# Pseudo-inverse of 128 landmark matrices on one core: one 64x64 tensor tile per head in place of block diagonals of two heads

## The chip, the cores and the metric

The kernel runs on one core of one Trainium2 chip. The metric is the time of one execution on the device in microseconds (us). The core's engines are TensorE (PE, its weight loads are listed apart as PEld), VectorE (DVE), ScalarE (ACT), GpSimd (POOL) and SyncE (SP, which here only starts transfers).

## The reference

The whole program is a two-dimensional LSTM over 16 images of 64x64 positions with 128 channels, then an attention layer with 64 landmarks and 8 heads of 16 channels, then a recurrent layer. The part that matters here is the pseudo-inverse of the landmark attention, one 64x64 matrix for each of 16 x 8 = 128 heads:

```python
def moore_penrose_pinv(x, iters=6):
    abs_x = jnp.abs(x)
    col = abs_x.sum(axis=-1).max()
    row = abs_x.sum(axis=-2).max()
    z = jnp.swapaxes(x, -1, -2) / (col * row)
    I = jnp.eye(x.shape[-1], dtype=x.dtype)
    for _ in range(iters):
        xz = x @ z
        z = 0.25 * z @ (13.0 * I - xz @ (15.0 * I - xz @ (7.0 * I - xz)))
    return z
attn2_inv = moore_penrose_pinv(attn2)
out = attn1 @ attn2_inv @ (attn3 @ v)
```

All of it is fp32. The maxima behind col and row go over all 128 heads.

## The kernel before

The program is a chain of phases, each an own block in which every engine has its own instruction queue: group norm, LSTM, landmark phase, pseudo-inverse (`pinv_phase`, L1080), output phase, recurrence. Engines wait for each other by semaphores alone, and the order on each engine is written out by hand.

`pinv_phase` holds the 128 matrices as NP = 64 pairs: partitions 0 to 63 carry the first head of a pair, 64 to 127 the second. They are worked on in NCH = 8 chunks of PCH = 8 pairs, so that a chunk of 64 columns per pair fills one bank of the matmul memory (PSUM). `bank` has four such banks, `wide` two times two for products of 128 columns per pair.

A matmul takes its weights over all 128 partitions. To multiply two heads in one 128x128 product, their matrices must stand on the diagonal of a 128x128 matrix that is otherwise zero. `diag_p` and `diag_t` are those matrices; `blocks(diag, c, h)` (L1136) is the part of a chunk that belongs to one head. Both are cleared at the start (L1153 on POOL, L1260 on DVE) and filled by copies, head by head.

Ahead of the rounds, in order: POOL makes `zeros` and `halves` (L1154 to L1158), and SP stores the zeros and eight diagonals for the next phase; TensorE sums the columns (L1169), DVE takes row sums and maxima (L1272 to L1276); ACT copies x into diag_p (L1235), TensorE turns it (L1179), ACT stores xT (L1239), DVE copies it into diag_t (L1280); POOL reduces the maxima over the partitions (L1160), DVE forms `inv` (L1286); TensorE multiplies xT by itself (L1188), ACT scales the product into `pz[..., 0, :]` (L1243) and x into `pz[..., 1, :]` (L1244), DVE copies the first into diag_p (L1291).

`pz` holds two matrices per head, P (which is x z) and a form of z, side by side in 128 columns. Each of the six rounds (PINV_ITERS, a loop on every engine) has three stages of eight chunks:

- stage 1: DVE forms 7 I - P in `tm` (L1300), TensorE multiplies by diag_p into `bank` (L1204);
- stage 2: DVE forms 15 I minus the bank in `tm` (L1303), TensorE multiplies by diag_p again (L1204);
- stage 3: DVE forms 3.25 I minus a quarter of the bank, in two instructions, straight into diag_t (L1307); TensorE multiplies both halves of pz by it into `wide` (L1215); ACT copies the result back to pz in two instructions per chunk (L1251) and its first half into diag_p in two more (L1255).

A stage's chunk c waits for the bank's reader four chunks earlier, and in stage 3 for ACT's copy of chunk c - 2. The copy into diag_p releases the next round's stage 1 by the semaphore s_pd. Behind the rounds TensorE multiplies each head's z by its context, with 64x64 weights and 16 columns, head by head (L1226), and DVE copies the result (L1312). Then the next phase's block begins.

Of the kernel before, what the change touches and what calls it, by code (L numbers as in the profile page):

```python
# [11 lines left out]
P = 128  # L12
# [1058 lines left out]
PCH = 8  # L1071
# [8 lines left out]
def pinv_phase(nc, sems, R, band, taps):  # L1080
# [7 lines left out]
    with ExitStack() as ctx:  # L1088
# [4 lines left out]
        diag_p = m.sb("i_diag_p", [P, NP, 2 * LM])  # L1093
        diag_t = m.sb("i_diag_t", [P, NP, 2 * LM])
# [16 lines left out]
        s_zero = sems.sem("i_zero")  # L1111
        s_zeros = sems.sem("i_zeros")
        s_band = sems.sem("i_band")
        s_xd = sems.sem("i_xd")
        s_xtd = sems.sem("i_xtd")
        s_pd = sems.sem("i_pd")
# [6 lines left out]
        s_pass = sems.sem("i_pass")  # L1123
# [11 lines left out]

        def blocks(diag, c, h):  # L1136
            return diag[HEAD[h], chunk[c], LM * h:LM * h + LM]
# [14 lines left out]
        def _(pool):  # L1152
            pool.memset(diag_p[:, :, :], 0.0).then_inc(s_zero, 1)  # L1153
# [9 lines left out]
        def _(pe):  # L1163
# [8 lines left out]
            for c in range(NCH):  # L1172
# [4 lines left out]
                pe.wait_ge(s_xd, c + 1)  # L1177
                for j in range(PCH):
                    mt = nc.tensor.matmul(bank[c % 4][:, j, :], diag_p[:, PCH * c + j, :], eye[1.0][:, :], start=True, stop=True)  # L1179
                mt.then_inc(s_x, 1)  # L1180

            for c in range(NCH):

                pe.wait_ge(s_xc, NCH + c - 3)
                pe.wait_ge(s_xtd, c + 1)
                for j in range(PCH):
                    n = PCH * c + j
                    mt = nc.tensor.matmul(bank[c % 4][:, j, :], diag_t[:, n, :], xT[:, n, :], start=True, stop=True)  # L1188
                mt.then_inc(s_x, 1)

            def iteration(k):
                for stage in range(2):
                    for c in range(NCH):


                        at = 3 * NCH * k + NCH * stage
                        pe.wait_ge(s_t, at + NCH + c - 3 if c >= 4 else at + c + 1 + 4 * stage)
                        pe.sem_inc(s_pass, 1)
                        if stage == 0:
                            pe.wait_ge(s_pd, NCH * k + c + 1)  # L1200
                            pe.sem_inc(s_pass, 1)
                        for j in range(PCH):
                            n = PCH * c + j
                            mt = nc.tensor.matmul(bank[c % 4][:, j, :], diag_p[:, n, :], tm[:, n, :], start=True, stop=True)  # L1204
                        mt.then_inc(s_q, 1)
                for c in range(NCH):
                    pe.wait_ge(s_t, 3 * NCH * k + 2 * NCH + c + 1)
                    pe.sem_inc(s_pass, 1)

                    pe.wait_ge(s_new, NCH * (k + 1) + c + 1)  # L1210
                    pe.sem_inc(s_pass, 1)
                    for j in range(PCH):
                        n = PCH * c + j
                        out = wide[c % 2][j // 4][:, j % 4, :, :].rearrange("p a l -> p (a l)")
                        mt = nc.tensor.matmul(out, diag_t[:, n, :], pz[:, n, :, :].rearrange("p a l -> p (a l)"),  # L1215
                                              start=True, stop=True)
                    mt.then_inc(s_pz, 1)
            pe.wait_ge(s_xc, 2 * NCH)
            with pe.Fori(0, PINV_ITERS) as k:
                iteration(k)  # L1220
# [976 lines left out]
```

## Time and profile before

| | us |
|---|---|
| median of 3 runs | 6811.03 |
| lowest and highest | 6809.58, 6813.49 |
| the profiled execution | 6810.61 |
| its span | 6808.7 |

The span goes from the first instruction to the last. Busy shares of the span are TensorE 91%, its weight loads 55%, VectorE 45%, ScalarE 47% and GpSimd 27%. The profile puts the pseudo-inverse at about 2674 to 3042 us of the span. Times in rows are us, or ns where a row says mean ns. "Idle before" is the time in which an engine stood still just ahead of the instructions of a group, with what ended it. PEclk is the clock that TensorE was granted as a share of 2.4 GHz. A matmul of fp32 appears as two weight loads and two matmul instructions, so that the 64 pairs of a stage are 128 of each. Rows name tiles without their numbers, and the form 64*64 is the rows and columns of the array that an instruction uses.

### The profile page before, as it was taken

Reading aid. Unit: us, or ns where it says so; the run is one execution under the profiler, and the core shown is the slowest. Engines: PE = TensorE matmul, PEld = TensorE weight load, DVE = VectorE, ACT = ScalarE, POOL = GpSimd, SP = SyncE. Lnnn points to the kernel's source line nnn. Section 1 sums busy time; section 2 is a strip of 40 time slices with the busy share of each in tenths; the row PEclk is TensorE's granted clock in tenths of the full one; section 3 lists DMA queues with packets and bytes.
Section 4 is the critical chain, followed back from the end, with each engine's and each line's share of the span. In section 5 each row is a group of like instructions: output and inputs, shape, how many; then the busy total and the mean of one; then the engine's idle time right before and its main releaser. Section 6 shows DMA issues by size and latency. Waiting matters only on the chain. (4 is left out here: it accounts for less than half of the span.)

```text
span 6808.7 us, 240684 instructions
## 1 busy us (share of the span) xinstructions
PE 6191.8 (91%) x100325; PEld 3736.2 (55%) x100560; DVE 3093.8 (45%) x8331; ACT 3215.1 (47%) x9215; POOL 1857.0 (27%) x2255
## 2 busy tenths in 40 slices
PE   4499999997888887989999999979999999999999
PEld 3499888995666665983444444433333333333333
DVE  7677777775777765434666666610000000000000
ACT  4366555564666664334555555523333333333333
POOL 1000000004767762005777777710000000000000
PEclk6699999998999999898999999989999999999999
DMA  6631112125766661014555555411111211211111
GB/s 265 257 115 67 69 50 75 58 102 178 218 216 205 206 201 38 0 33 127 154 155 154 155 157 154 127 54 44 55 44 43 56 43 43 56 43 47 52 44 42
DMA packets 785139, 715.35 MB, mean 105 GB/s; under 512 B 68336, under 2 KB 662256, under 8 KB 781040
## 3 DMA queue, kind: packets, MB, share of 16 engines
q1 hardware_dynamic: 769712, 599.13, 28.7%
q0 software_dynamic: 14400, 101.45, 3.7%
q8 instruction: 776, 12.71, 0.8%
q14 instruction: 251, 2.06, 0.1%
HBM read 390.60 MB, written 307.89 MB: 103 GB/s over the span
## 5 line engine op out<-in xcount | busy, mean ns | idle before, releaser
L2096 PE MATMUL f_junk<-f_idle 128*32 128x384 bf16 x24736 | 1566.7, 323 | 2.4 <-issue 2.4
L2139 ACT ACTIVATE f_y<-f_acc 128x16 f32<-128x16 f32 x4096 | 753.7, 184 | 1553.8 <-PE f_acc L2107 1553.8
L2107 PEld LDWEIGHTS f_acc<-f_y,f_vT 128*32 128x32 f32 x32768 | 649.2, 108 | 1412.1 <-ACT f_y L2139 1401.1
L2107 PE MATMUL f_acc<-f_y,f_vT 128*32 128x16 f32 x32768 | 1049.7, 193 | 58.0 <-issue 9.5
L2054 DVE TENSOR_TENSOR f_sum<-f_turned,f_t 128x512 f32<-128x512 f32 x128 | 88.5, 691 | 1762.9 <-PE f_turned L2089 1762.9
L1826 DVE TENSOR_REDUCE o_m<-o_bank_l 128x8 f32<-128x512 f32 x512 | 325.6, 678 | 382.0 <-remote 372.8
L2096 PEld LDWEIGHTS f_junk<-f_idle 128*32 128x32 bf16 x24736 | 447.0, 96 | 4.5 <-issue 4.2
L399 ACT ACTIVATE l_gate<-l_pf,l_bf 128x256 f32<-128x256 f32 (+12 forms) x768 | 273.4, 407 | 229.0 <-PE l_pf L374 228.4
L336 POOL DMA_DIRECT2D hidden<-l_h x48 | 36.2, 754 | 1256.9 <-DVE l_hsum L453 1191.9
L916 ACT ACTIVATE a_p<-a_s 128x512 f32<-128x512 f32 x512 | 264.3, 602 | 194.0 <-PE a_s L807 194.0
L365 PE MATMUL l_pf<-l_x,l_wf 128*128 128x256 f32 (+12 forms) x1536 | 317.9, 330 | 36.7 <-DMA l_x<-skew 36.7
L1792 ACT ACTIVATE o_p<-o_bank_s 128x512 f32<-128x512 f32 x512 | 264.4, 602 | 88.2 <-PE o_bank_s L1647 88.2
L365 PEld LDWEIGHTS l_pf<-l_x,l_wf 128*128 128x128 f32 x1536 | 253.0, 191 | 52.4 <-issue 36.8
L402 ACT ACTIVATE l_tanhc<-l_cell 128x256 f32<-128x256 f32 (+12 forms) x384 | 137.3, 358 | 277.3 <-DVE l_cell L429 277.3
L976 DVE TENSOR_REDUCE a_m3p<-a_s 128x1 f32<-128x512 f32 x384 | 238.2, 682 | 53.4 <-remote 51.8
L2044 DVE TENSOR_SCALAR f_wxn<-f_wx,f_scale,f_shift 128x2048 f32<-128x2048 f32 x32 | 84.9, 2652 | 384.3 <-DMA f_wx<-wx 344.2
L2089 PE MATMUL f_turned<-f_ident,f_y 128*32 128x128 f32 x4096 | 224.3, 292 | 1.7 <-issue 1.5
L2078 PE MATMUL f_acc<-f_wxn,f_ident 128*32 128x128 f32 x4096 | 211.1, 278 | 15.2 <-DVE f_wxn L2044 13.3
L701 POOL TENSOR_TENSOR a_r<-a_vare,a_half 128x8 f32<-128x8 f32 x128 | 209.6, 1638 | 10.0
L434 DVE TENSOR_TENSOR l_h<-l_gate,l_tanhc 128x256 f32<-128x256 f32 (+12 forms) x384 | 134.3, 350 | 163.0 <-ACT l_tanhc L402 163.0
L1204 PE MATMUL i_bank<-i_tm,i_diag_p 128*128 128x64 f32 x1536 | 198.3, 299 | 2.7 <-DVE i_tm L1300 2.7
L1204 PEld LDWEIGHTS i_bank<-i_tm,i_diag_p 128*128 128x128 f32 x1536 | 198.0, 215 | 2.8 <-issue 2.8
(253 smaller groups left out, 12939.2 us busy)
## 6 DMA issues: line engine op xcount, KB each, us to landing
a_hid<-hidden SPq DMA_DIRECT2D x112, 520.0 KB, 4.6
hidden<-l_h POOLq DMA_DIRECT2D x48, 1040.0 KB, 6.4
skew<-gn_skew POOLq DMA_DIRECT2D x8, 6144.0 KB, 23.8
l_x<-skew SPq DMA_DIRECT2D x48, 1024.0 KB, 5.2
vals<-a_v SPq DMA_DIRECT2D x128, 272.0 KB, 3.0
o_v<-vals SPq DMA_DIRECT2D x128, 272.0 KB, 3.5
gn_x<-in_x SPq DMA_DIRECT2D x16, 2048.0 KB, 12.4
a_xin<-in_x SPq DMA_DIRECT2D x128, 256.0 KB, 4.4
```

Of the source, the lines that this page charges most:

```text
L365: mm = nc.tensor.matmul(banks[c][g][:, :, rows], w[W[g]][:, :], xs, start=g in (0, 2, 3), stop=False, skip_group_check=True)
L399: nc.scalar.activation(gate[c][:, g, :, rows], banks[c][g][:, :, rows], ACT.Tanh if g == 2 else ACT.Sigmoid, bias=bias[BI[g]][:, 0:1]).the ...
L916: nc.scalar.activation(p3[c % 2][g][:, :], S[g][:, :], ACT.Exp).then_inc(s["exp"], 1)
L976: nc.vector.tensor_reduce(m3p[:, g, c:c + 1], bank[:, :], AX.X, ALU.max).then_inc(s["mx"], 1)
L1204: mt = nc.tensor.matmul(bank[c % 4][:, j, :], diag_p[:, n, :], tm[:, n, :], start=True, stop=True)
L1792: nc.scalar.activation(p1[g][:, :], bank_s[g][:, :], ACT.Exp).then_inc(s["exp"], 1)
L1826: nc.vector.tensor_reduce(m1[:, k, :].rearrange("p (g r) -> p g r", r=QUAD)[:, :, 0:2], bank_l[k % 2][:, :].rearrange("p (g a l) -> p g a ...
L2078: mm = nc.tensor.matmul(acc[k % 2][rows, PT * piece:PT * piece + PT, :], ident[:, rows], wxn[q][:, at, :], start=piece == 0, stop=False, s ...
L2089: mt = nc.tensor.matmul(turned[g % 2][rows, b % 4, :], y[q][:, rows, b], ident[:, :], start=True, stop=True)
L2096: nc.tensor.matmul(junk[rows, :], idle[:, 0:QUAD], idle[:, :], start=True, stop=True)
L2107: mm = nc.tensor.matmul(acc[k % 2][rows, t, :], vT[:, rows], before, start=False, stop=True, skip_group_check=True)
L2139: nc.scalar.activation(y[q][:, u, :], acc[u // RC % 2][:, u % RC, :], ACT.Sigmoid).then_inc(s_y, 1)
```

## The change

The diagonals go. Each product of a pair becomes two matmuls, one for each head, whose weights are 64x64: the first head uses rows 0 to 63 and columns 0 to 63 of the array, the second the other rows and columns. The weights are read directly from x, xT, pz and a new tile `tq`. All clearings and copies of the diagonals and their semaphores (s_zero, s_xd, s_xtd, s_pd, and s_pass) are removed; stage 1 waits for ACT's copy of pz (s_new) in place of s_pd. DVE's third instruction of a round becomes one over 128 partitions. The loops over rounds on the three engines are written out, and the last round forms only the second half of pz (`first`).

```diff
@@ -1090,8 +1090,7 @@
         xT = m.sb("i_xT", [P, NP, LM])
         pz = m.sb("i_pz", [P, NP, 2, LM])
         tm = m.sb("i_tm", [P, NP, LM])
-        diag_p = m.sb("i_diag_p", [P, NP, 2 * LM])
-        diag_t = m.sb("i_diag_t", [P, NP, 2 * LM])
+        tq = m.sb("i_tq", [P, NP, LM])
...
@@ -1150,7 +1141,6 @@
 
         @block.gpsimd
         def _(pool):
-            pool.memset(diag_p[:, :, :], 0.0).then_inc(s_zero, 1)
             pool.memset(zeros[:, :, :], 0.0).then_inc(s_zeros, 1)
             pool.memset(halves[:, :], 0.0).then_inc(s_const, 1)
             pool.wait_ge(s_const, 1)
@@ -1174,50 +1164,46 @@
                     pe.wait_ge(s_col, NCH + c - 3)
                 else:
                     pe.wait_ge(s_xc, c - 3)
-                pe.wait_ge(s_xd, c + 1)
                 for j in range(PCH):
-                    mt = nc.tensor.matmul(bank[c % 4][:, j, :], diag_p[:, PCH * c + j, :], eye[1.0][:, :], start=True, stop=True)
+                    for h in HEAD:
+                        mt = nc.tensor.matmul(bank[c % 4][h, j, :], x[h, PCH * c + j, :], eye[1.0][h, :], start=True, stop=True)
                 mt.then_inc(s_x, 1)
 
             for c in range(NCH):
 
                 pe.wait_ge(s_xc, NCH + c - 3)
-                pe.wait_ge(s_xtd, c + 1)
                 for j in range(PCH):
                     n = PCH * c + j
-                    mt = nc.tensor.matmul(bank[c % 4][:, j, :], diag_t[:, n, :], xT[:, n, :], start=True, stop=True)
+                    for h in HEAD:
+                        mt = nc.tensor.matmul(bank[c % 4][h, j, :], xT[h, n, :], xT[h, n, :], start=True, stop=True)
                 mt.then_inc(s_x, 1)
 
-            def iteration(k):
+            pe.wait_ge(s_xc, 2 * NCH)
+            for k in range(PINV_ITERS):
                 for stage in range(2):
                     for c in range(NCH):
 
-
                         at = 3 * NCH * k + NCH * stage
                         pe.wait_ge(s_t, at + NCH + c - 3 if c >= 4 else at + c + 1 + 4 * stage)
-                        pe.sem_inc(s_pass, 1)
                         if stage == 0:
-                            pe.wait_ge(s_pd, NCH * k + c + 1)
-                            pe.sem_inc(s_pass, 1)
+                            pe.wait_ge(s_new, 2 + NCH * k + c + 1)
                         for j in range(PCH):
                             n = PCH * c + j
-                            mt = nc.tensor.matmul(bank[c % 4][:, j, :], diag_p[:, n, :], tm[:, n, :], start=True, stop=True)
+                            for h in HEAD:
+                                mt = nc.tensor.matmul(bank[c % 4][h, j, :], pz[h, n, 0, :], tm[h, n, :], start=True, stop=True)
                         mt.then_inc(s_q, 1)
+                first = 1 if k == PINV_ITERS - 1 else 0
                 for c in range(NCH):
                     pe.wait_ge(s_t, 3 * NCH * k + 2 * NCH + c + 1)
-                    pe.sem_inc(s_pass, 1)
 
                     pe.wait_ge(s_new, NCH * (k + 1) + c + 1)
-                    pe.sem_inc(s_pass, 1)
                     for j in range(PCH):
                         n = PCH * c + j
-                        out = wide[c % 2][j // 4][:, j % 4, :, :].rearrange("p a l -> p (a l)")
-                        mt = nc.tensor.matmul(out, diag_t[:, n, :], pz[:, n, :, :].rearrange("p a l -> p (a l)"),
-                                              start=True, stop=True)
+                        for h in HEAD:
+                            mt = nc.tensor.matmul(wide[c % 2][j // 4][h, j % 4, first:2, :].rearrange("p a l -> p (a l)"),
+                                                  tq[h, n, :], pz[h, n, first:2, :].rearrange("p a l -> p (a l)"),
+                                                  start=True, stop=True)
                     mt.then_inc(s_pz, 1)
-            pe.wait_ge(s_xc, 2 * NCH)
-            with pe.Fori(0, PINV_ITERS) as k:
-                iteration(k)
 
             pe.wait_ge(s_new, 2 + NCH * (PINV_ITERS + 1))
             for n in range(NP):
@@ -1229,11 +1215,6 @@
         @block.scalar
         def _(act):
             act.sem_inc(s_new, 2)
-            act.wait_ge(s_zero, 2)
-            for c in range(NCH):
-                for h in range(2):
-                    mc = nc.scalar.activation(blocks(diag_p, c, h), x[HEAD[h], chunk[c], :], ACT.Identity)
-                mc.then_inc(s_xd, 1)
             for c in range(NCH):
                 act.wait_ge(s_x, NCH + c + 1)
                 nc.scalar.activation(xT[:, chunk[c], :], bank[c % 4][:, :, :], ACT.Identity).then_inc(s_xc, 1)
@@ -1243,21 +1224,17 @@
                 nc.scalar.activation(pz[:, chunk[c], 0, :], bank[c % 4][:, :, :], ACT.Identity, scale=inv[:, 0:1]).then_inc(s_xc, 1)
                 nc.scalar.activation(pz[:, chunk[c], 1, :], x[:, chunk[c], :], ACT.Identity, scale=inv[:, 0:1]).then_inc(s_new, 1)
 
-            with act.Fori(0, PINV_ITERS) as k:
+            for k in range(PINV_ITERS):
+                first = 1 if k == PINV_ITERS - 1 else 0
                 for c in range(NCH):
                     act.wait_ge(s_pz, NCH * k + c + 1)
                     for h in range(2):
                         lo = PCH * c + 4 * h
-                        mc = nc.scalar.activation(pz[:, lo:lo + 4, :, :], wide[c % 2][h][:, :, :, :], ACT.Identity)
+                        mc = nc.scalar.activation(pz[:, lo:lo + 4, first:2, :], wide[c % 2][h][:, :, first:2, :], ACT.Identity)
                     mc.then_inc(s_new, 1)
-                    act.wait_ge(s_new, 2 + NCH * (k + 1) + c + 1)
-                    for h in range(2):
-                        mc = nc.scalar.activation(blocks(diag_p, c, h), pz[HEAD[h], chunk[c], 0, :], ACT.Identity)
-                    mc.then_inc(s_pd, 1)
 
         @block.vector
         def _(dve):
-            nc.vector.memset(diag_t[:, :, :], 0.0).then_inc(s_zero, 1)
             steps = 0
 
             def step(ins):
@@ -1274,27 +1251,16 @@
             for c in range(NCH):
                 dve.wait_ge(s_x, c + 1)
                 nc.vector.tensor_reduce(cmax[:, c:c + 1], flat(bank[c % 4][:, :, :]), AX.X, ALU.max).then_inc(s_col, 1)
-            for c in range(NCH):
-                dve.wait_ge(s_xc, c + 1)
-                for h in range(2):
-                    mc = nc.vector.tensor_copy(blocks(diag_t, c, h), xT[HEAD[h], chunk[c], :])
-                mc.then_inc(s_xtd, 1)
             dve.wait_ge(s_col, NCH)
             step(nc.vector.tensor_reduce(top[:, 1:2], cmax[:, :], AX.X, ALU.max))
             dve.wait_ge(s_all, 1)
             step(nc.vector.tensor_tensor(prod[:, :], tops[:, 0:1], tops[:, 1:2], ALU.mult))
             step(nc.vector.reciprocal(inv[:, :], prod[:, :]))
 
-            for c in range(NCH):
-                dve.wait_ge(s_xc, NCH + c + 1)
-                for h in range(2):
-                    mc = nc.vector.tensor_copy(blocks(diag_p, c, h), pz[HEAD[h], chunk[c], 0, :])
-                mc.then_inc(s_pd, 1)
-
-            def both(k, rows=slice(0, P)):
-                return eye[k][rows, :].unsqueeze(1).broadcast_to([rows.stop - rows.start, PCH, LM])
-
-            with dve.Fori(0, PINV_ITERS) as k:
+            def both(k):
+                return eye[k][:, :].unsqueeze(1).broadcast_to([P, PCH, LM])
+
+            for k in range(PINV_ITERS):
                 for c in range(NCH):
                     dve.wait_ge(s_new, 2 + NCH * k + c + 1)
                     nc.vector.tensor_tensor(tm[:, chunk[c], :], both(7.0), pz[:, chunk[c], 0, :], ALU.subtract).then_inc(s_t, 1)
@@ -1303,10 +1269,8 @@
                     nc.vector.tensor_tensor(tm[:, chunk[c], :], both(15.0), bank[c % 4][:, :, :], ALU.subtract).then_inc(s_t, 1)
                 for c in range(NCH):
                     dve.wait_ge(s_q, 2 * NCH * k + NCH + c + 1)
-                    for h in range(2):
-                        mc = nc.vector.scalar_tensor_tensor(out=blocks(diag_t, c, h), in0=bank[c % 4][HEAD[h], :, :], scalar=-0.25,
-                                                            in1=both(3.25, HEAD[h]), op0=ALU.mult, op1=ALU.add)
-                    mc.then_inc(s_t, 1)
+                    nc.vector.scalar_tensor_tensor(out=tq[:, chunk[c], :], in0=bank[c % 4][:, :, :], scalar=-0.25,
+                                                   in1=both(3.25), op0=ALU.mult, op1=ALU.add).then_inc(s_t, 1)
             dve.wait_ge(s_z, 1)
             for q in range(2):
                 nc.vector.tensor_copy(c3[:, 32 * q:32 * q + 32, :].rearrange("p n d -> p (n d)"),
```

## Rows read from the trace of the kernel before

**Rows 1.** The page's first lines: span, and busy time with its share and instructions.

```profile
span 6808.7 us, 240684 instructions
PE 6191.8 (91%) x100325; PEld 3736.2 (55%) x100560; DVE 3093.8 (45%) x8331; ACT 3215.1 (47%) x9215; POOL 1857.0 (27%) x2255
```

**Rows 2.** Timeline at both ends of the phase: start, duration, engine, line, operation, count, idle before.

```profile
2673.93 6.93 POOL L1153 MEMSET i_diag_p<- 128x8192 f32 x1 [49.07 <-POOLq L502]
2675.72 6.88 DVE L1260 MEMSET i_diag_t<- 128x8192 f32 x1 [2.07 <-issue]
...
2682.78 10.10 PE L1169 MATMUL i_bank<-r_attn,i_halves 128*128 128x512 f32 x16 [9.60 <-POOL i_halves L1158]
...
2692.71 14.40 PE L1179 MATMUL i_bank<-i_eye,i_diag_p 128*128 128x64 f32 x128
...
2709.83 0.69 ACT L1243 ACTIVATE i_pz<-i_bank,i_inv 128x512 f32<-128x512 f32 x1 [2.09 <-DVE i_inv L1286]
...
2711.03 0.68 ACT L1243 ACTIVATE i_pz<-i_bank,i_inv 128x512 f32<-128x512 f32 x1
...
2724.13 2.16 PE L1204 MATMUL i_bank<-i_tm,i_diag_p 128*128 128x64 f32 x9 [2.73 <-DVE i_tm L1300]
...
3040.95 1.29 DVE L1312 COPY r_ctx<-i_bank 128x512 f32<-128x512 f32 x2 [30.98 <-PE i_bank L1226]
```

**Rows 3.** Groups by line and form, 2675.5 to 3042 us; the first line names the columns.

```profile
line engine op names shapes xcount | busy us, mean ns | idle before us <-releasers
L1204 PE MATMUL i_bank<-i_tm,i_diag_p 128*128 128x64 f32 x1536 | 198.3, 299 | 2.7 <-DVE i_tm L1300 2.7
...
L1215 PE MATMUL i_wide<-i_pz,i_diag_t 128*128 128x128 f32 x768 | 95.2, 280 | 9.9 <-ACT i_pz L1251 9.3
...
L1307 DVE SCALAR_TENSOR_TENSOR i_diag_t<-i_bank,i_eye 64x512 f32<-64x512 f32 x96 | 66.1, 689 | 36.9 <-PE i_bank L1204 36.2
L1255 ACT ACTIVATE i_diag_p<-i_pz 64x512 f32<-64x512 f32 x96 | 60.4, 629 | 2.1
L1251 ACT ACTIVATE i_pz<-i_wide 128x512 f32<-128x512 f32 x96 | 52.1, 594 | 192.4 <-PE i_wide L1215 191.4
L1300 DVE TENSOR_TENSOR i_tm<-i_eye,i_pz 128x512 f32<-128x512 f32 x48 | 32.6, 691 | 69.0 <-ACT i_pz L1251 69.0
...
L1226 PE MATMUL i_bank<-r_ctx,i_pz 64*64 64x16 f32 x256 | 12.5, 251 | 2.7 <-ACT i_pz L1251 2.7
```

**Rows 4.** Chosen stretches with busy time and granted clock; the first line names the columns.

```profile
core 0: us, PE busy (x) PEld busy (x) DVE busy (x) ACT busy (x) POOL busy (x), PEclk, DMA share, GB/s
...
2724.20:2778.60 54.40, 54.40 (x256) 54.40 (x256) 18.80 (x29) 0.00 (x0) 0.00 (x0) 0.50 0.00 1
2778.80:2785.20 6.40, 6.40 (x49) 6.39 (x48) 2.07 (x3) 3.29 (x6) 0.00 (x0) 0.83 0.01 3
2798.00:2823.00 25.00, 25.00 (x226) 25.00 (x225) 13.95 (x22) 3.03 (x6) 0.00 (x0) 1.00 0.00 0
...
3030.20:3040.80 10.60, 10.60 (x202) 10.60 (x200) 0.00 (x0) 0.00 (x0) 0.00 (x0) 0.50 0.01 2
3063.40:3090.80 27.40, 27.40 (x45) 4.98 (x46) 0.00 (x0) 4.18 (x7) 0.00 (x0) 0.50 0.36 97
```

**Rows 5.** Timeline of two chunks of stage 3, and of the final product.

```profile
2787.89 2.02 PE L1215 MATMUL i_wide<-i_pz,i_diag_t 128*128 128x128 f32 x16 [0.39 <-ACT i_pz L1251]
...
2790.30 2.02 PE L1215 MATMUL i_wide<-i_pz,i_diag_t 128*128 128x128 f32 x16 [0.39 <-ACT i_pz L1251]
...
3028.42 12.48 PE L1226 MATMUL i_bank<-r_ctx,i_pz 64*64 64x16 f32 x256 [2.71 <-ACT i_pz L1251]
```

**Rows 6.** Timeline of the landmark phase: four tiles side by side.

```profile
2657.63 1.06 PE L807 MATMUL a_s<-a_qbd,a_kT 32*128 32x128 f32 x32
2658.62 1.10 PE L821 MATMUL a_pv<-a_p,a_v 128*32 128x64 f32 x64
```

More of the change, by code:

```diff
@@ L1110, in pinv_phase @@
         zeros = m.sb("i_zeros", [P, HEADS, BAND])
-        s_zero = sems.sem("i_zero")
         s_zeros = sems.sem("i_zeros")
         s_band = sems.sem("i_band")
-        s_xd = sems.sem("i_xd")
-        s_xtd = sems.sem("i_xtd")
-        s_pd = sems.sem("i_pd")
         s_x = sems.sem("i_x")
@@ L1122, in pinv_phase @@
         s_new = sems.sem("i_new")
-        s_pass = sems.sem("i_pass")
         s_z = sems.sem("i_z")
@@ L1134, in pinv_phase @@
         HEAD = [slice(0, LM), slice(LM, 2 * LM)]
-        def blocks(diag, c, h):
-            return diag[HEAD[h], chunk[c], LM * h:LM * h + LM]
         @block.sync
```

## The prediction

> **What bounds the kernel now.** The span is 6808.7 us, TensorE is busy for 91% of it, and one core runs the phases one after another [rows 1]. The change touches the pseudo-inverse alone, which lies between DVE's clearing of a diagonal tile at 2675.72 and the two copies of the result at 3040.95 [rows 2], 365 us or 5.4% of the span. Whatever moves inside moves the end by as much, because the next phase starts behind it and does the same work. So the first view is the list of groups by line in this stretch [rows 3], then the stretches with the granted clock [rows 4], then the timeline [rows 2, 5, 6].
>
> The list says who works: L1204 (two of the three stages of a round) and L1215 (the third) keep TensorE busy for 198.3 and 95.2 us, with 2.7 and 9.9 us of idle time [rows 3]. From the first L1204 (2724.13) to L1226 (3028.42) it is 304.3 us [rows 2, 5]. In a stage of L1204, TensorE is the bound. A product of fp32 is two instructions, so a stage is 64 pairs x 2 = 128 of them, and they follow at 25.00 us / 224 = 0.112 us with a clock of 1.00 (226 less the two in progress at an edge), and at 54.40 / 256 = 0.213 us with 0.50 [rows 4]: 14.3 and 27.2 us a stage. In a stage of L1215 the matmuls would take 14.3 us too, but a chunk comes only every 2.41 us (2787.89 to 2790.30) [rows 5], because ACT makes two copies of 0.594 and then two into the diagonal of 0.629 us per chunk [rows 3]: ACT is the bound there, 8 x 2.41 = 19.3 us.
>
> The clock is the second thing to see. After TensorE's pause of 2.7 us [rows 3] ahead of the rounds it was granted 0.50, that is 1.2 of 2.4 GHz, and stayed there through the first two stages, 54.4 us without a gap; it rose as soon as L1215 ran (mean 0.83 in 2778.8 to 2785.2), and then stayed at 1.00 in L1204 as well [rows 4].
>
> **Stages 1 and 2 of a round.** Each pair's product of 128x128 by 64 becomes two of 64x64 by 64, in different rows and columns of the array: 256 instructions in place of 128. The nearest row is L1226, already in this form but with 16 columns. There 202 instructions stand in 10.60 us at clock 0.50 [rows 4]; less the four in progress that is 99 pairs, 0.107 us for the two heads together. At clock 1.00 the row is L821, four tiles with 64 columns side by side: 64 instructions in 1.10 us, of which 0.22 is the tail of the last, so 16 slots (15 gaps) of 0.058 us [rows 6]. A slot holds one pass of both heads, and a stage has 128: 128 x 0.058 = 7.4 us at the high clock, 128 x 0.107 = 13.7 us at the low. This halves the stage at either clock, since 64 columns of weights are loaded in place of 128.
>
> **Stage 3.** Here each head streams 128 columns, so the slot is bound by the stream. L807 has this width with four tiles: 32 instructions in 1.06 us, 0.27 of it tail, so seven gaps of 0.112 [rows 6]. The stage is 14.3 us at the high clock, and at the low 128 x 0.213 = 27.2 us. ACT's two diagonal copies are gone, which leaves two of 0.594 = 1.2 us per chunk under TensorE's 1.8: the ACT bound goes and TensorE is next. In the last round the left half is dropped: 64 columns, 7.4 or 13.7 us. DVE has 0.69 us per chunk and stage (the third now one instruction over 128 partitions in place of two over 64, same elements per partition, 0.689 each) [rows 3], under the 0.93 of a chunk of 16 slots; no new wait. At the turn of a round DVE's first stage waits for ACT's last copy, about 2.1 us behind the last L1215, and the fifth chunk, which needs DVE beyond that, starts only 3.7 us behind: hidden. If that cover went, it would cost about 1 us a round.
>
> **Rounds, summed.** High clock: 5 x (7.4 + 7.4 + 14.3) + 3 x 7.4 = 167.7 us; with some 5 us at the low clock first and small seams, 171.5. That is 132.8 less than 304.3. Low clock throughout: 5 x (13.7 + 13.7 + 27.2) + 3 x 13.7 = 314.1 us, 9.8 more than now.
>
> **Before the rounds.** TensorE's first product waits for POOL's small constants, queued behind the clearing of diag_p, and starts at 2682.78 [rows 2]. Without it they are ready some 6.8 us sooner: 2676.0 (bounds: nothing gained beyond DVE's own start at 2675.72, and 1.5 us lost if other work ends later). The products of L1169 take 9.9 us as now, to 2685.9. The transposes (L1179, 128 instructions in 14.40 us [rows 2]) take 128 x 0.058 = 7.5, to 2693.4. In the next step (L1188) ACT is late: its two scaled copies per chunk follow at 2711.03 - 2709.83 = 1.20 us [rows 2] against 0.93 on TensorE, so the last is done at 2694.5 + 7 x 1.20 + 0.69 = 2703.6. The 16+16+16 copies into diagonals and two clearings lie off this path. Rounds start at 2703.7, not 2724.13: 20.4 us gained (bounds 14 and 24). The price is a pause of about 4 us for TensorE ahead of the rounds, longer than the 2.7 us after which the clock was low; so I take it that the rounds start at the low clock again.
>
> **Behind the rounds.** The pause of 2.7 us before L1226 [rows 3], mostly ACT's queue, shrinks to 1.0: 1.7 gained. L1226 itself (12.48 us [rows 5]) is unchanged; with the clock high a little longer I take 11, between 7.5 and 13.7: 1.5 gained. The rounds written out take more code; TensorE ran L1179 and L1226 from straight code without a gap, so nothing for that (bounds 0 and 3 us). Fewer copies on ACT, DVE and POOL gain nothing else.
>
> **Forecast.** Profiled time 6810.6 - 20.4 - 132.8 - 1.7 - 1.5 = 6654.2; the median of the runs is 0.4 above the profiled one, so 6655 us. It stands on the clock rising early in the rounds.
>
> **Rival 1: the clock stays low.** Nothing here shows what two 64x64 tiles side by side do to the clock. For a rise: in the new stages both tiles stream nearly all the time (64 columns streamed while 64 weights load), where the old L1204 streamed half the time. Against: together they fill half the array, now in stage 3 too, and that was the stage that raised the clock. In 3063.4 to 3090.8 TensorE alternated full 128x512 matmuls with pairs of 32x32 tiles, was never idle, and kept 0.50 for 27.4 us [rows 4], so streaming alone does not do it; whether rows, columns or their product count, those rows leave open. If it stays low: 6810.6 - 20.4 + 9.8 - 1.7 + 1.2 (L1226 all low) = 6799.5, within 0.2% of now. The Trainium skill, TensorE: Matmul & The Clock Gate, Part 1, says that the clock goes by how busy TensorE has been of late, idle time lowering it and activity raising it. By that alone the forecast would be sure; the 54.4 us at 0.50 with no idle time [rows 4] speak against so simple a reading.
>
> **Rival 2: the heads go one after another, and it is slower.** L1226's tiles stream 16 columns, a small part of a slot, so its rows do not prove that two long streams into the same bank overlap. L807 writes four banks; L821 writes one bank from tiles in different columns with all rows. If the two heads' streams excluded each other, each slot would double: 1664 x 0.058 (13 stages of 128 slots) + 640 x 0.112 (5 stages) = 168 us in the rounds and 14 in the steps before. That gives 6655 + 182 = 6837 with the high clock, and more with the low. It decides for slower from 156/182 = 86% of the doubling on. The Trainium skill, TensorEngine Tiling (Array Packing), Gotcha 1: PSUM Pressure, has this rule: different row tiles cannot access the same PSUM bank at the same time. The two heads are different row tiles and share a bank, in different partitions; L1226 shows starts in pairs at one slot [rows 4], which speaks against it.
>
> **Rival 3: the clock wavers**, rising in some rounds only: about 6720 us.
>
> **How the numbers follow.** Forecast 0.50, rival 1 0.38, rival 2 0.05, rival 3 0.03; 0.04 for rival 1 with 2304 slots each over 0.011 us dearer, which alone would pass 6824. The forecast's own range is 6642 to 6672; rival 1's is 6793 to 6812. To hold eight in ten the range must take in both: 6642 to 6812. About 0.2%, 13.6 us, is what a measurement of this kernel can tell from no change. Faster by more: 0.50 + 0.03 and part of rival 1's lower end, 0.55. Within: 0.36. Slower: 0.09.
>
> **What would show it.** The first stages' slots in the new profile: 0.058 us (two instructions each) and a clock of 1.00 for the forecast, 0.107 and 0.50 for rival 1; starts of the two heads apart by a whole stream for rival 2. Stage 3: chunks 1.8 us apart, with ACT idle between. Rounds starting some 28 us behind the phase's start. A wait of TensorE for DVE within stages 1 and 2 would make the prediction wrong in a way that I have not priced.

## The result, and the profile after

The changed kernel takes 6652.85 us (median of four runs, 6649.13 to 6655.99) against 6810.31 for the kernel before in the same comparison: a ratio of 0.9771, with a 95% interval of 0.9757 to 0.9786. The forecast was 6655. The profiled execution took 6654.42 us, its span is 6652.8.

The first lines of the page, as [rows 1]:

```profile
span 6652.8 us, 245191 instructions
PE 6083.1 (91%) x103120; PEld 3601.9 (54%) x103120; DVE 3042.8 (46%) x8250; ACT 3140.9 (47%) x9103; POOL 1851.7 (28%) x2254
```

155.9 us of span are gone, and TensorE's share is the same 91%, which by itself says nothing. The groups by line of the pseudo-inverse are the answer to [rows 3]. L1193 is the old L1204, L1203 the old L1215, L1233 the old L1251, L1266 and L1272 the old L1300 and L1307, L1212 the old L1226.

```profile
line engine op names shapes xcount | busy us, mean ns | idle before us <-releasers
L1193 PE MATMUL i_bank<-i_tm,i_pz 64*64 64x64 f32 x3072 | 90.6, 218 | 2.6 <-ACT i_pz L1224 2.6
...
L1203 PE MATMUL i_wide<-i_pz,i_tq 64*64 64x128 f32 x1280 | 70.7, 269 | 0.0
L1233 ACT ACTIVATE i_pz<-i_wide 128x512 f32<-128x512 f32 x80 | 43.4, 594 | 101.9 <-PE i_wide L1203 101.9
L1266 DVE TENSOR_TENSOR i_tm<-i_eye,i_pz 128x512 f32<-128x512 f32 x48 | 33.3, 693 | 59.3 <-ACT i_pz L1233 47.8 <-ACT i_pz L1225 11.5
L1272 DVE SCALAR_TENSOR_TENSOR i_tq<-i_bank,i_eye 128x512 f32<-128x512 f32 x48 | 33.2, 692 | 11.6 <-PE i_bank L1193 11.6
...
L1212 PE MATMUL i_bank<-r_ctx,i_pz 64*64 64x16 f32 x256 | 10.4, 232 | 0.7 <-ACT i_pz L1233 0.7
...
L1203 PE MATMUL i_wide<-i_pz,i_tq 64*64 64x64 f32 x256 | 8.3, 219 | 0.0
```

Twice as many instructions of stages 1 and 2 (3072 for 1536) take 90.6 us in place of 198.3, of which 54.4 were at the low clock [rows 4]. No engine holds TensorE up inside the rounds: its only idle time is the 2.6 us ahead of them and the 0.7 behind. VectorE's third instruction over 128 partitions costs the same 0.69 us as each of the two over 64 partitions did, so a chunk of stage 3 saves one of the two.

The stretches with the granted clock, as [rows 4]:

```profile
core 0: us, PE busy (x) PEld busy (x) DVE busy (x) ACT busy (x) POOL busy (x), PEclk, DMA share, GB/s
2703.20:2717.80 14.60, 14.60 (x506) 14.60 (x504) 10.81 (x16) 0.36 (x1) 0.00 (x0) 1.00 0.02 4
2718.20:2732.00 13.80, 13.80 (x258) 13.80 (x256) 5.30 (x8) 7.59 (x14) 0.00 (x0) 1.00 0.01 2
...
2872.00:2875.50 3.50, 3.50 (x126) 3.50 (x125) 0.00 (x0) 0.00 (x0) 0.00 (x0) 1.00 0.00 0
2876.00:2881.80 5.80, 5.80 (x114) 5.80 (x112) 0.00 (x0) 0.00 (x0) 0.00 (x0) 0.50 0.00 0
```

A slot is, as in the prediction, the time for one instruction of each head. In stages 1 and 2, 506 instructions less some eight in progress are 249 pairs in 14.60 us: 0.0586 us a slot. In stage 3, 258 less four are 127 pairs in 13.80 us: 0.109. Read start by start, the second head's instruction of stages 1 and 2 begins 0.006 to 0.007 us behind the first head's, and the next pair 0.051 to 0.052 us later, so the two do run together. The clock is at 1.00 from the first instruction of the rounds to their end, where the kernel before had 54.4 us at 0.50 [rows 4]. It falls to 0.50 in the final product, whose pairs of 64x64 tiles stream 16 columns, without any idle time there.

The timeline, as [rows 2, 5], with two chunks of stage 3 on ScalarE:

```profile
2673.26 1.38 POOL L1144 MEMSET i_zeros<- 128x1536 f32 x1 [49.07 <-POOLq L502]
...
2675.24 10.05 PE L1159 MATMUL i_bank<-r_attn,i_halves 128*128 128x512 f32 x16 [2.75 <-POOL i_halves L1148]
...
2685.22 7.68 PE L1169 MATMUL i_bank<-i_eye,r_attn 64*64 64x64 f32 x256
...
2692.74 7.63 PE L1178 MATMUL i_bank<-i_xT 64*64 64x64 f32 x256
...
2703.00 15.15 PE L1193 MATMUL i_bank<-i_tm,i_pz 64*64 64x64 f32 x512 [2.63 <-ACT i_pz L1224]
...
2725.18 1.08 ACT L1233 ACTIVATE i_pz<-i_wide 128x512 f32<-128x512 f32 x2 [0.66 <-PE i_wide L1203]
2726.93 1.08 ACT L1233 ACTIVATE i_pz<-i_wide 128x512 f32<-128x512 f32 x2 [0.66 <-PE i_wide L1203]
...
2871.58 10.45 PE L1212 MATMUL i_bank<-r_ctx,i_pz 64*64 64x16 f32 x256 [0.75 <-ACT i_pz L1233]
2882.07 1.29 DVE L1276 COPY r_ctx<-i_bank 128x512 f32<-128x512 f32 x2 [18.64 <-PE i_bank L1212]
```

| part | before | after | difference | forecast |
|---|---|---|---|---|
| POOL's first instruction to the first round | 50.2 | 29.7 | -20.5 | -20.4 |
| rounds, with the wait behind them | 304.3 | 168.6 | -135.7 | -134.5 |
| the final product, to DVE's copy | 12.5 | 10.5 | -2.0 | -1.5 |
| all else | | | +2.3 | 0 |

The last line is the rest up to the 155.9 us. The phases on either side do the same work, and here they were 0.7 us shorter ahead of the pseudo-inverse and 3.0 us longer behind it. Such differences come between executions of one kernel too: the kernel before took 6810.31, 6809.4, 6806.05 and 6804.04 us (medians) in the four comparisons of this document. Differences of totals from different comparisons are therefore good to some 5 us, and smaller terms are read from the traces.

### The profile page after: what moved, and what is told of

It reads as the page before. It is cut to its first block and busy times, and to the rows that moved or that the text cites. A ratio compares the mean times of both kernels' runs of the same rounds, so it can differ in the third digit from the quotient of the medians.

```text
span 6652.8 us, 245191 instructions
## 1 busy us (share of the span) xinstructions
PE 6083.1 (91%) x103120; PEld 3601.9 (54%) x103120; DVE 3042.8 (46%) x8250; ACT 3140.9 (47%) x9103; POOL 1851.7 (28%) x2254
## 5 line engine op out<-in xcount | busy, mean ns | idle before, releaser
L336 POOL DMA_DIRECT2D hidden<-l_h x48 | 36.3, 756 | 1256.0 <-DVE l_hsum L453 1191.1
L373 PE MATMUL l_pf<-l_h,l_uf 128*128 128x256 f32 (+12 forms) x768 | 196.5, 337 | 0.7
L1726 ACT ACTIVATE o_res<-o_bank_s 128x512 f32<-128x512 f32 x128 | 76.5, 597 | 241.7 <-PE o_bank_s L1633 241.7
```

## The experiments

Two things were not settled by the result. The rounds began at the high clock, so that rival 1 was never put to the test. And a gain of 136 us in the rounds is one sum of several terms. Unless said otherwise, a run is compared with the changed kernel's 6652.85 us; ratios are to the kernel before in the same comparison.

**What the tiles do to a clock that is low.** The changed kernel, with a pause made long enough:

```diff
+            pe.wait_ge(s_pause, 3)
             for k in range(PINV_ITERS):
...
                     nc.vector.tensor_tensor(tm[:, chunk[c], :], both(7.0), pz[:, chunk[c], 0, :], ALU.subtract).then_inc(s_t, 1)
+                if k == 0:
+                    for i in range(3):
+                        nc.vector.memset(tq[:, :, :], 0.0).then_inc(s_pause, 1)
+                        dve.wait_ge(s_pause, i + 1)
```

> The changed kernel with three clearings of the tile tq on VectorE (10 to 11 us, of no use) between the first 7 I - P and the rounds, and TensorE waits for the last. TensorE's pause ahead of the rounds grows from 2.6 to about 14 us, so the rounds should start at a granted clock of 0.50; in the changed kernel they started at 1.00 and so never put the question. Theory (two 64x64 tiles side by side raise the clock): it rises within the first 10 us of the rounds, 6652.9 + 12 + 2 to 5 = 6667 to 6670 us. Rival (they do not): 0.50 through all six rounds, slots of 0.107 and 0.213 us, 314 us in place of 168, so about 6812 us, the time of the kernel before.

It took 6665.64 us, ratio 0.9791 (0.9774 to 0.9807), 1.4 us under the theory's range. Stretches of its trace:

```profile
2702.00:2715.90 13.90, 0.00 (x0) 0.00 (x0) 11.10 (x4) 0.12 (x1) 0.00 (x0) 0.51 0.00 0
2716.20:2719.30 3.10, 3.10 (x62) 3.10 (x62) 0.69 (x1) 0.00 (x0) 0.00 (x0) 0.50 0.02 5
2719.50:2732.30 12.80, 12.80 (x446) 12.80 (x443) 9.51 (x14) 0.00 (x0) 0.00 (x0) 1.00 0.01 4
```

The pause became 17.1 us. The rounds start at 0.50, with 62 instructions in 3.10 us, and are at 1.00 within 3.5 us. Pairs of 64x64 tiles raised the clock, where 128x128 products of the same 64 columns had not in 54.4 us [rows 4]. Rival 1 falls: the first two stages took 16.5 us in place of 15.0, so a low start costs 1.5 us, not 146.

**The same tiles, not side by side.**

```diff
-                        for j in range(PCH):
-                            n = PCH * c + j
-                            for h in HEAD:
+                        for h in HEAD:
+                            for j in range(PCH):
+                                n = PCH * c + j
```

and likewise in stage 3 (one of two places shown).

> The changed kernel with the loops over heads and pairs exchanged in the three stages: within a chunk all products of the first head are issued, then all of the second, so that no neighbours lie in different tiles. Same instructions, same data. Theory (the halving comes from the two heads standing side by side): each instruction takes a slot alone, 2304 slots become 4608, + 168 us at the high clock, 6821 us, and up to 7000 if the clock is low in part of it, since each tile then streams alone. Rival (the halving comes from loading 64 columns of weights in place of 128, whatever the order): TensorE pulls the two together anyhow, no change, 6653 us.

It took 6970.32 us, ratio 1.0236 (1.0219 to 1.0253): slower than the kernel before, by about as much as the change had made it faster. Stretches of stages 1 and 2 and of stage 3 in the first round, and the timeline of two chunks of stage 3:

```profile
2702.00:2742.00 40.00, 40.00 (x481) 40.00 (x480) 10.35 (x15) 0.00 (x0) 0.00 (x0) 0.50 0.01 2
2743.00:2783.00 40.00, 40.00 (x245) 40.00 (x244) 5.38 (x8) 7.60 (x14) 0.00 (x0) 0.50 0.00 1
```

```profile
2749.61 10.68 PE L1203 MATMUL i_wide<-i_pz,i_tq 64*64 64x128 f32 x64
```

The theory's direction is right. Its 6821 us for the high clock is short by 149; it had also named up to 7000 for a low clock, and a low clock is what came. The clock was 1.00 when the rounds began (2700.44 us), fell 1.5 us later to 0.50 although TensorE had no gap, and stayed there for the 486 us up to the end of the rounds and on into the next phase. One tile after the other, through one half of the rows and one half of the columns, kept TensorE busy all the time and did not bring the clock up.

An instruction takes 0.083 us on average (40.00 / 481) in stages 1 and 2, where a pair side by side takes 0.107 at this clock, and 0.163 in stage 3. So the theory's slot for each instruction alone holds only in part. Read start by start, nine of 16 instructions in stages 1 and 2 follow the one before by 0.107 us, and seven follow closer, by 0.006 to 0.101. This comes once in every 16 instructions, as often as the head changes: there neighbours lie in different tiles, and some of them still overlap.

The order of two loops is worth 317 us here. What the order costs at the high clock no run shows. An estimate of the split: by the prediction's price the rounds with pairs take 314 us when the clock stays low, which is 146 more than the 168.6 measured; the rounds with the heads apart took 488.5, another 174.

**The clock's share of the gain.** The kernel before, with TensorE's pause of 2.7 us filled by three matmuls whose result nobody uses:

```diff
+            for i in range(3):
+                nc.tensor.matmul(wide[0][0][:, :, :, :].rearrange("p a b l -> p (a b l)"), halves[:, :], flat(x[:, chunk[i], :]), start=True, stop=True)
             pe.wait_ge(s_xc, 2 * NCH)
             with pe.Fori(0, PINV_ITERS) as k:
```

> The kernel before with three matmuls of 128x128 by 512 fp32 (into a bank that is free, result unused, 2.6 us at the high clock) in TensorE's pause of 2.7 us ahead of the rounds. Theory (that pause let the clock fall, and the first two stages then stayed at 0.50): the rounds start at 1.00, stages 1 and 2 of the first round take 28.6 us in place of 54.4, so 6810.3 - 26 = 6784 us. This is the part of the change's gain that comes by the clock and not by the tiles. Rival (the length of the run of half-filled matmuls lets it fall, not the pause): it falls somewhere in stage 1, 6805 to 6811 us.

It took 6783.8 us against 6809.4, ratio 0.996 (0.9946 to 0.9975):

```profile
2727.10:2729.80 2.70, 2.70 (x7) 0.92 (x6) 1.82 (x4) 1.30 (x2) 0.00 (x0) 1.00 0.00 0
2730.00:2758.00 28.00, 28.00 (x252) 28.00 (x252) 18.38 (x29) 0.00 (x0) 0.00 (x0) 1.00 0.00 1
```

The three matmuls save 25.6 us, as expected. In the kernel before the clock fell within the pause, 1.5 us after TensorE's last instruction; here it did not. The 128x128 products of stages 1 and 2 hold a high clock for 28 us, and did not raise a low one in 54.4 us [rows 4]. This is a gain that the kernel before had open, and a part of what the change brought.

**The tiles alone.** The kernel before with `part(diag, n, h)`, the 64x64 block of a diagonal tile, as the weights of two products per pair in all four places, of which one is shown; copies, waits and loops stay:

```diff
-                            mt = nc.tensor.matmul(bank[c % 4][:, j, :], diag_p[:, n, :], tm[:, n, :], start=True, stop=True)
+                            for h in range(2):
+                                mt = nc.tensor.matmul(bank[c % 4][HEAD[h], j, :], part(diag_p, n, h), tm[HEAD[h], n, :], start=True, stop=True)
```

> The kernel before with one part of the change: each product of a pair becomes two of 64x64 whose weights are read from the blocks of the diagonal tiles. All clearings, copies, waits and loops stay. Theory (the tiles halve stages 1 and 2 and bring the clock up; stage 3 stays with ScalarE): rounds 6 x (7.5 + 7.5 + about 18) + a few us = about 200 in place of 304, and some 8 us of the two products ahead of the rounds, so 6809 - 104 - 8 = about 6697 us. Rival (without dropping the copies the tiles bring little, since ScalarE's copies set the pace of the round): rounds over 260 us, above 6760 us.

It took 6699.28 us, ratio 0.9844 (0.9829 to 0.9859). Its rounds went from 2714.0 to 2919.0, 205 us. The start of the rounds, and a stretch of stage 3:

```profile
2714.10:2719.10 5.00, 5.00 (x96) 5.00 (x98) 4.93 (x9) 0.00 (x0) 0.00 (x0) 0.50 0.01 3
2719.30:2731.00 11.70, 11.62 (x392) 11.43 (x390) 9.94 (x15) 0.00 (x0) 0.00 (x0) 1.00 0.02 4
2735.00:2745.00 10.00, 8.48 (x144) 7.63 (x141) 4.61 (x7) 9.73 (x17) 0.00 (x0) 1.00 0.01 2
```

The low start comes of itself here, after a pause of 5.5 us, and is over in 5.2 us. In stage 3 ScalarE is busy for 9.73 of 10 us: the old bound is still there. Against 6806.05 us of the kernel before in this comparison the tiles alone are 107 us, of the change's 157. The 26 us of the clock are among them.

**ScalarE's copies.** The changed kernel with the two copies per chunk back in the first five rounds; stage 1 waits for them (s_pd), which the lines shown leave out:

```diff
                     mc.then_inc(s_new, 1)
+                    if k < PINV_ITERS - 1:
+                        act.wait_ge(s_new, 2 + NCH * (k + 1) + c + 1)
+                        for h in range(2):
+                            mc = nc.scalar.activation(diag_p[HEAD[h], chunk[c], LM * h:LM * h + LM], pz[HEAD[h], chunk[c], 0, :], ACT.Identity)
+                        mc.then_inc(s_pd, 1)
```

> The changed kernel with ScalarE's two copies per chunk into a diagonal tile put back in stage 3 of the first five rounds (the tile is read by nobody; stage 1 waits for the copy, as in the kernel before). Theory (ScalarE bound stage 3 before, and taking it off that path is worth 5 us a round): chunks of stage 3 are 2.4 us apart instead of 1.75, + 5 x 5.2 = 26 us, 6679 us. Rival (with matmuls of half the length elsewhere the copies would find room, and the gain is all in the matmuls): under 8 us, at most 6661 us.

It took 6670.52 us (6665.20 to 6677.77), ratio 0.9794 (0.9778 to 0.9811), between the theory's 6679 and the rival's 6661. ScalarE's timeline in stage 3, then TensorE's:

```profile
2727.49 1.08 ACT L1237 ACTIVATE i_pz<-i_wide 128x512 f32<-128x512 f32 x2
2728.61 1.27 ACT L1242 ACTIVATE i_diag_p<-i_pz 64x512 f32<-64x512 f32 x2
2729.91 1.08 ACT L1237 ACTIVATE i_pz<-i_wide 128x512 f32<-128x512 f32 x2
```

```profile
2726.31 1.96 PE L1207 MATMUL i_wide<-i_pz,i_tq 64*64 64x128 f32 x32 [0.20 <-ACT i_pz L1237]
2728.72 1.97 PE L1207 MATMUL i_wide<-i_pz,i_tq 64*64 64x128 f32 x32 [0.45 <-ACT i_pz L1237]
```

Chunks are 2.4 us apart again (1.75 without the copies), but the rounds take 186.6 us, 18.0 more and not 26. The first three chunks of a stage run without a wait, and only the other five are paced by ScalarE: a stage 3 takes 17.0 us in place of 14.0. TensorE goes on to stage 1 while the last copies still run, and the next two stages take 0.6 us more. The copies cost 3.6 us a round.

**The loops.** The changed kernel with the three `Fori` loops put back, the increments of s_pass between TensorE's waits that stood in the kernel before, and with the loops the full last round:

> The changed kernel with its three loops over rounds put back (and with them both halves of pz formed in the last round, since a loop has one body). Theory (writing out gains nothing by itself, the half left out is worth one half stage): + 14.3 - 7.5 = 7 us, 6660 us. Rival (loops cost something at each turn): more than 10 us, above 6663 us.

It took 6664.62 us, ratio 0.9792 (0.9777 to 0.9807). By the total the rival would have it, by the trace it does not. The rounds take 177.3 us, 8.7 more, and this execution began them at the low clock:

```profile
2700.70:2704.00 3.30, 3.30 (x65) 3.30 (x67) 1.36 (x2) 0.00 (x0) 0.00 (x0) 0.51 0.02 5
```

The first round is 2.4 us longer than in the changed kernel, of which the low clock in stages 1 and 2 makes 2.0. The last one is 6.3 us longer: that is the half left out. The four rounds between take 28.9 us each, with loops as without, so writing out is worth nothing. The two profiled executions differ by 9.0 us in all; that the medians differ by 11.8 lies outside the pseudo-inverse and within what separates one comparison from another.

**The clearings.** The changed kernel with both back at the head of their queues, on tiles that nobody reads:

```diff
+            pool.memset(diag_p[:, :, :], 0.0)
             pool.memset(zeros[:, :, :], 0.0).then_inc(s_zeros, 1)
...
+            nc.vector.memset(diag_t[:, :, :], 0.0)
```

> The changed kernel with the two clearings of 128x8192 put back at the head of GpSimd's and VectorE's queues (of tiles that nobody reads). Theory (they delayed the first product and the row sums by their 6.9 us, and nothing else covered that): + 7, 6660 us, rounds starting 7 us later behind the end of the landmark phase. Rival (only a part of it is on the path): + 0 to 3.

It took 6658.08 us (6652.59 to 6659.68), ratio 0.978 (0.9765 to 0.9795), 5 us more; the totals alone would not tell 5 from 3 or 7. The trace does:

```profile
2669.17 6.93 POOL L1146 MEMSET i_diag_p<- 128x8192 f32 x1 [46.53 <-POOLq L502]
...
2678.01 2.93 PE L1162 MATMUL i_bank<-r_attn,i_halves 128*128 128x512 f32 x3 [9.60 <-POOL i_halves L1151]
```

From POOL's first instruction to the first product it is 8.8 us, as before the change (2673.93 to 2682.78 [rows 2]), against 2.0 without the clearing: 6.9 us. From POOL's first instruction to the first round it is 36.3 against 29.7, so 6.6 of them reach the rounds, and the rival (0 to 3) falls. Both clearings went back together; VectorE's alone was not tried.

**A version that beats both.** The clock rose under the full 128x128 products of 128 columns of L1215, and the first image's convolutions in the next phase (full 128x512 products alternating with 32x32 ones) left it low for 27.4 us [rows 4]. Ahead of them TensorE stands idle for transfers. The changed kernel, with 14 matmuls there whose result nobody uses:

```diff
         def _(pe):
+            def fill(times):
+                for _ in range(times):
+                    nc.tensor.matmul(bank_y[:, :], R.ident[:, :], R.attn2[:, 0:2, :, :].rearrange("p b g l -> p (b g l)"), start=True, stop=True)
+            fill(4)
             pe.wait_ge(s["w"], 64)
...
                 queries(0, c)
+            fill(10)
             pe.wait_ge(s_band, 16)
```

> The changed kernel with 14 matmuls of 128x512 fp32 of no use in the output phase: four before TensorE's first wait and ten between the first two products and the first convolution, where it stands idle for transfers at a clock of 0.50 for 68 us in all. The first experiments showed that a clock once low stays low under the mix of full and small products that follows, and rises under full ones. Theory: the clock is back at 1.00 before the first convolution, whose eight steps of 3.8 us take some 2.4, - 11 to - 14 us, about 6640 us. Rival (the matmuls outlast the transfers or the first image waits for other engines): within 3 us of 6653 or later.

It took 6635.18 us (6632.04 to 6647.34), ratio 0.9757 (0.9744 to 0.977): 17.7 us less, and two of its five runs lay 12 above the others. So both kernels ran once more, on one chip (e9_after_again and e10_filled_again, meant for this, gave no result):

> The changed kernel as it is, for a comparison on one chip with the version of it that has the 14 matmuls in the output phase. Theory: 6653 us as in its first runs, within 4 us.

> The changed kernel with the 14 matmuls in the output phase once more, beside the changed kernel on the same chip. Theory (the first image's convolutions at the high clock): 13 to 18 us below the changed kernel, so that the two intervals against the kernel before do not overlap. Rival (the first difference of 17.7 us was mostly that of two chips or sets of runs): less than 8 us.

The changed kernel took 6647.15 us (6645.69 to 6649.02), ratio 0.9769 (0.9755 to 0.9782), 2 us outside what was expected of it; with the matmuls 6631.32 (6626.18 to 6637.12), ratio 0.9746 (0.9733 to 0.976). The difference is 15.8 us, within the expected 13 to 18. The two intervals against the kernel before were not to overlap, and they do at their ends; but no run of the one kernel reaches a run of the other. Both timelines, first without and then with them:

```profile
2900.68 2.07 PE L1628 MATMUL o_bank_s<-o_v,o_bands 128*128 128x512 f32 x2 [8.16 <-DMA o_bands<-band]
2904.47 2.08 PE L1628 MATMUL o_bank_s<-o_v,o_bands 128*128 128x512 f32 x2
```

```profile
2890.53 8.75 PE L1577 MATMUL o_bank_y<-r_attn,r_ident 128*128 128x512 f32 x20
2899.65 1.12 PE L1632 MATMUL o_bank_s<-o_v,o_bands 128*128 128x512 f32 x2 [0.37 <-DMA o_bands<-band]
...
2901.65 1.17 PE L1632 MATMUL o_bank_s<-o_v,o_bands 128*128 128x512 f32 x2
```

The clock, first in the changed kernel's own profile, then with the matmuls:

```profile
2889.00:2943.90 54.90, 43.15 (x84) 8.78 (x88) 5.16 (x8) 8.63 (x15) 4.29 (x6) 0.50 0.48 133
```

```profile
2901.00:2917.00 16.00, 15.72 (x47) 3.17 (x44) 0.30 (x1) 4.78 (x8) 0.00 (x0) 1.00 0.67 186
```

The filling ends 0.4 us before the transfer that it covers, and a convolution takes 2.0 to 2.1 us in place of 3.8. Eight of them are 14 us.

## Why the prediction was right, point by point

**Slots.** 0.058 us was forecast for stages 1 and 2 and 0.0586 measured; 0.112 for stage 3, and 0.109 measured. Both came from rows of four tiles in another phase [rows 6], one with as many streamed columns and one with the same width of stage 3. (The row behind the first gives 0.88 / 15 = 0.0587, which the prediction has as 0.058.) The sum of the rounds at the high clock, 167.7 us, stands against 167.8 measured up to TensorE's last instruction of the rounds; stages 1 and 2 were 0.07 us longer each than 7.4, a full stage 3 was 0.3 shorter than 14.3 and the last one 0.9 longer than 7.4, so that the sum fits to 0.1 is in part luck.

**Where the gain in the rounds lies.** The two timelines split the 135.7 us by stage. The low clock of the first two stages, 54.6 us in place of the 28.5 of every later round, is 26.1 (filled pause: 25.6). The tiles in stages 1 and 2 are 6 x (28.53 - 14.94) = 81.5. Stage 3 of five rounds is 17.1 (18.2 and four times 17.2, down to 14.0 each; ScalarE's copies put back: 18.0). The last stage 3 with the wait behind it, 20.0 down to 9.1, is 11.0. The prediction had all four inside two totals, and one reading on the way was wrong: it gave a stage 3 of the kernel before 8 x 2.41 = 19.3 us, but only its later chunks come 2.41 apart, and it took 17.2. The sum did not use that figure, since it started from the measured 304.3.

**One sum was wrong.** The 304.3 us reach to the start of L1226 and so hold the wait of 2.7 ahead of it, while the 171.5 are added up from the stages. The 132.8 thus has the wait's gain in it already, and the 1.7 "behind the rounds" takes it off a second time. Put right, rounds and wait were forecast at 171.5 + 1.0 = 172.5 us; 168.6 were measured. The other side of it is a low start of 2.5 us and seams of 1.3, neither of which is in the profiled execution. The two errors nearly cancel, which leaves 134.5 against 135.7: luck, of some 3 us.

**Ahead of the rounds.** -20.5 for -20.4, but one step inside was wrong: "The price is a pause of about 4 us for TensorE ahead of the rounds". By the prediction's own figures TensorE is done at 2693.4 + 7.5 = 2700.9, and rounds at 2703.7 leave 2.8; the pause was 2.63, and L1178 ran its 7.63 us without idle time. The start of the rounds is set by ScalarE's eight copies either way, so the sum held. Nor do "two clearings lie off this path": GpSimd's was on it, as the same paragraph says first, and the run with both put back moved the rounds by 6.6 us. The low start that the 4 us were to bring did not come in the profiled execution. It came in others and cost 1.5 us in the repeated changed kernel and 2.0 in the one with loops.

**The range.** 6642 to 6812 held the forecast and rival 1, so that 6652.85 lies in it says little. It also lies in the forecast's own 6642 to 6672. The forecast had even odds, because nothing ahead of it showed what the pairs do to the clock; that part was a bet, and the paused kernel is what shows it to be right.

**Rival 1** had 0.38. The argument against a rise was that two tiles fill only half the array. The paused kernel shows that they raise the clock, and the kernel with the heads apart shows that one tile at a time does not. The paused kernel also shows rival 1's slot of 0.107 us (62 instructions less four in progress, in 3.10 us): its price for stages 1 and 2 was right, its condition was not met. The Trainium skill, TensorE: Matmul & The Clock Gate, Part 1, has activity raise the clock and idle time lower it; read by the busy column, this trace does not agree, since the kernel with the heads apart had TensorE busy without a gap for 486 us at 0.50.

**Rival 2** named a danger that exists, with another cause: its 6837 was for streams that exclude each other in one bank, and the heads issued apart took 6970. The two heads do write one bank at the same time, and no penalty shows, so the rule on row tiles and banks (the Trainium skill, TensorEngine Tiling (Array Packing), Gotcha 1) does not show for different partitions of a bank: 249 pairs in 14.60 us. What can undo the change is the order of issue.

**Cover.** The seams named as hidden were hidden: within the rounds no wait of TensorE appears in the groups. The written-out code cost nothing, and gained nothing beyond the half stage. What the copies of the diagonals on VectorE and ahead of the rounds cost by themselves was not tried.

## What to carry to other kernels

In this kernel two independent products of 64 rows and 64 columns were better issued as two tiles next to each other than as one block-diagonal product: a slot fell from 0.112 to 0.0586 us at the high clock, and the copies into the diagonal went. The two had to be neighbours in the queue; with the loops the other way round the kernel became slower than it had been. And look at the granted clock of a stage before pricing it: a pause of 2.7 us halved the speed of the 54 us behind it, and three matmuls into a free bank during that pause gave 25.6 us back. Such filling is cheap to try.

## What the runs showed of the hardware

- A stream of 128x128 products with 64 columns held a clock of 1.00 for 28 us when it began there, and held 0.50 for 54.4 us when it began there. Pairs of 64x64 tiles with 64 columns went from 0.50 to 1.00 within 3.4 to 5.2 us of their start (paused kernel, loops, tiles alone). The same tiles issued head by head, most of them one at a time, fell from 1.00 to 0.50 after 1.5 us and stayed there for 486 us. What in the tiles makes the difference stays open, and no run here separates it.
- Pairs of 64x64 tiles with only 16 columns (the final product) did not hold a high clock: it fell to 0.50 within them in the changed kernel and again when that was repeated, with no idle time in between, and it was at 0.50 from 1.7 us on in the kernel before.
- After the same pause of 2.6 us one execution of the changed kernel kept 1.00 throughout the rounds. Another began them at 1.00, fell to 0.50 after 1.4 us of gapless work and was back at 1.00 after another 3.4 us. What decides between the two was not found.
- Two tiles in different rows, columns and partitions wrote one bank at the same time, 0.006 to 0.007 us apart in their starts, at 0.0586 us for the two.
- An instruction of VectorE over 64 partitions took 0.689 us and one over 128 partitions 0.692, with 512 elements per partition each.
